# Attention with a relation bias: score matmuls moved from 128-row to 64-row TensorE tiles

## What is computed

```python
attn_scores = jnp.einsum('bihd,bjhd->bhij', q, k) / scale
li = x @ rel_W[:, :d].T
lj = x @ rel_W[:, d:].T
logits = li[:, :, None, :] + lj[:, None, :, :] + rel_b
relation_probs = jax.nn.softmax(logits, axis=-1)
bias = jnp.einsum('bijk,hk->bhij', relation_probs, logical_bias)
attn_scores = attn_scores + gate * bias
attn_weights = jax.nn.softmax(attn_scores, axis=-1)
out = jnp.einsum('bhij,bjhd->bihd', attn_weights, v)
```

## Time and profile before

| | |
|---|---|
| median of three runs | 5008.73 us |
| the profiled execution | 5018.32 us, its span 5016.4 us |
| busy PE, DVE, ACT, POOL | 89%, 76%, 67%, 41% |
| mean DMA rate over the span | 114 GB/s |
| PE instructions (matmul, weight load) | 74128, 74128 |

### The profile page before, as it was taken

One profiled execution on the slowest core, in us unless ns is written; L12 is line 12 of the kernel. 1 busy time (PEld: TensorE's weight loads), 2 busy tenths in 40 slices (PEclk: granted clock), 3 DMA queues, 4 the chain that ended last, 5 costly groups with the idle time before them and its releaser, 6 DMA issues. The chain is left out here.

```text
span 5016.4 us, 183232 instructions
## 1 busy us (share of the span) xinstructions
PE 4458.2 (89%) x74128; PEld 3458.1 (69%) x74128; DVE 3821.7 (76%) x6309; ACT 3380.7 (67%) x4458; POOL 2057.0 (41%) x1809
## 2 busy tenths in 40 slices
PE   6459999999999999999999999999999996289992
PEld 3227777777777777777777777777777785267771
DVE  4388888888888888888888888888888843167773
ACT  2017887888787788877877787888888882044440
POOL 0114444444444444444444444444444442433335
PEclk9659999999999999999999999999999998589996
DMA  7514544544555445554454455454554456244434
GB/s 96 82 33 112 118 113 111 118 112 115 113 112 112 111 114 116 113 118 110 114 114 112 109 113 116 113 119 115 115 114 111 112 114 178 79 146 149 150 137 113
DMA packets 496919, 573.65 MB, mean 114 GB/s; under 512 B 136360, under 2 KB 369704, under 8 KB 492096
## 3 DMA queue, kind: packets, MB, share of 16 engines
q1 hardware_dynamic: 486880, 543.96, 46.5%
q0 software_dynamic: 6144, 16.79, 1.1%
q10 hardware_dynamic: 3040, 0.98, 0.1%
HBM read 305.10 MB, written 46.65 MB: 70 GB/s over the span
## 5 line engine op out<-in xcount | busy, mean ns | idle before, releaser
L734 DVE TENSOR_REDUCE b_mxp<-b_mx 128x1 f32<-128x512 f32 x4096 | 2635.4, 686 | 559.0 <-PE b_mx L835 508.9
L703 ACT ACTIVATE b_pr<-b_sc 128x1024 f32<-128x1024 f32 x2048 | 1986.5, 1021 | 697.0 <-PE b_sc L824 689.2
L814 PE MATMUL b_sc<-b_qm,kst 128*128 128x128 f16 x16384 | 1272.3, 220 | 54.3 <-ACT b_pr L703 42.0
L824 PE MATMUL b_sc<-b_cm,b_rst 112*128 112x128 f16 x16384 | 1264.5, 220 | 42.8 <-DMA b_rst<-b_rhi 35.5
L814 PEld LDWEIGHTS b_sc<-b_qm,kst 128*128 128x128 f16 x16384 | 971.6, 98 | 283.7 <-issue 229.5
L860 PE MATMUL b_acc<-b_pr,vp 128*32 128x128 f32 x32768 | 1124.1, 277 | 27.3 <-issue 26.9
L824 PEld LDWEIGHTS b_sc<-b_cm,b_rst 112*128 112x128 f16 x16384 | 1012.0, 98 | 49.4 <-DMA b_rst<-b_rhi 40.4
L860 PEld LDWEIGHTS b_acc<-b_pr,vp 128*32 128x32 f32 x32768 | 839.2, 110 | 265.2 <-ACT b_pr L703 190.2
L636 POOL TENSOR_TENSOR b_ex<-b_ex 128x512 f32<-128x512 f32 x512 | 654.7, 1279 | 680.8 <-ACT b_ex L682 680.8
L835 PE MATMUL b_mx<-kst,b_qx 64*128 64x512 f16 x4096 | 819.4, 397 | 92.1 <-DVE b_mxp L734 76.9
L642 POOL CAST b_rhi<-b_ex 128x512 f16<-128x512 f32 x512 | 312.8, 611 | 1293.0 <-ACT b_ex L690 1244.5
(11 more groups left out here) (144 smaller groups left out, 1726.0 us busy)
## 6 DMA issues: line engine op xcount, KB each, us to landing
b_dj<-key_logits SPq DMA_DIRECT2D x256, 768.0 KB, 7.9
b_rst<-b_rhi SPq DMA_DIRECT2D x2048, 64.0 KB, 3.2
b_rst<-b_rlo SPq DMA_DIRECT2D x1024, 64.0 KB, 3.1
c_w1r<-in_L_ffn_W_dram SPq DMA_DIRECT2D x23, 1024.0 KB, 4.9
c_w2r<-in_L_ffn_W_dram SPq DMA_DIRECT2D x23, 1024.0 KB, 4.8
expert_tokens<-c_zeros SPq DMA_DIRECT2D x23, 512.0 KB, 6.8
c_xb<-expert_tokens SPq DMA_DIRECT2D x23, 512.0 KB
expert_results<-c_y SPq DMA_DIRECT2D x23, 512.0 KB, 2.9
```

What stands on the lines that cost most here:

```text
L703: nc.scalar.activation(pr[:, jt % 2, half, :], sc[:, half].rearrange("p a b -> p (a b)"), ACT.Exp).then_inc(s["p_ready"], 1)
L734: nc.vector.tensor_reduce(mxp[:, head, part:part + 1], mx[:, (bank + ab) % MX_RING, :], AX.X, ALU.max).then_inc(s["mx_used"], 1)
L814: pe.matmul(sc[:, half, side, p * P:p * P + P], kst[:, pair, jt * P:jt * P + P], qm[:, par, :, pair, side * IS:side * IS + IS], start=(p = ...
L824: ins = pe.matmul(out, rst[:, u % 2, b, j0:j0 + P], cm[:, par, half, b], start=False, stop=(b % (NB // 2) == NB // 2 - 1), skip_group_chec ...
```

## The change

The score part of a step is cut differently. The products use 64-row tiles: head a of a pair on rows 0 to 63, head b on rows 64 to 127, each matmul with 64 moving columns (half of the queries), 32 matmuls a step; q is no longer padded with zeros. The relation part is also on 64 rows: 16 groups of 4 rows (three parts and a row of ones) for 8 queries, again 32 matmuls a step with 64 columns, one 64-row tile for each half of the queries. The halves of ACT's Exp are now even and odd heads. The relation matmuls come first, each half behind `p_ready`, then all products; the second half of the products waits on a new semaphore `relation_done`; `scores_ready` rises twice at the very end. `pe_pv` runs in one go behind both halves.

Around it: the relation logits for both terms come as two rows for each half of the partitions, so `dj` is 512 KB a unit and the two 512-wide Exp become one 1024-wide Exp; `sp_r` has 6 copies of 128 KB a unit, spread over rows at a step of 4 partitions, and issued in three portions that wait for `scores_ready` at steps 0, 1 and 2 of the unit; the coefficient map has 512 columns on 128 partitions instead of 1024 on 112; `pool_sum` runs ahead of `pool_c` and `pool_parts` behind it; the q copies move to units 2 and 3; the constants of a chunk take 11 DMAs instead of 4, and the bound 2 instead of 1. Token order is plain, so loads and stores of 8 DMAs become one each, and the 48 stores of `c_values` become 4.

```diff
-NB, BI = 8, 16
+NB, BI = 8, 8
+PARTS = 4
-C_MAPS = (12, 13)
+C_MAPS = (13, 14)
...
-                for b in range(NB):
-                    sp.dma_start(x[BI * b:BI * b + BI, 8 * q:8 * q + 8, :],
-                                 by_block(hidden)[b // 4, b % 4, :, 8 * q:8 * q + 8, :]).then_inc(x_in[q], 16)
+                sp.dma_start(x[:, 8 * q:8 * q + 8, :],
+                             hidden.rearrange("o (t p) d -> (o p) t d", p=P)[:, 8 * q:8 * q + 8, :]).then_inc(x_in[q], 16)
...
-            for part, t in ((0, chi), (1, chi), (2, clo)):
+            for part, t in enumerate((chi, clo)):
                 for k in range(2):
-                    for b in range(NB):
-                        sp.dma_start(c_dram[:, part, k].rearrange("x (i b) h -> b i x h", b=NB)[b],
-                                     t[BI * b:BI * b + BI, k]).then_inc(stored, 16)
+                    sp.dma_start(c_dram[part].rearrange("a k i x h -> k a i (x h)")[k],
+                                 t[:, k].rearrange("p x h -> p (x h)")).then_inc(stored, 16)
...
-        dj = sb("dj", [P, 2, 3, JU])
-        rst = sb("rst", [ROWS, 2, NB, JU], F16)
-        qm = sb("qm", [P, 2, 2, PAIRS, P], F16)
-        cm = sb("cm", [ROWS, 2, 2, NB, HH, BI], F16)
+        dj = sb("dj", [P, 2, 2, JU])
+        rst = sb("rst", [P, 2, NB, JU], F16)
+        qm = sb("qm", [P, 2, PAIRS, P], F16)
+        cm = sb("cm", [P, 2, 2, NB, PAIRS, BI], F16)
...
-            sp.dma_start(cval[0:M_ROW, par].rearrange("r b h -> r (b h)"),
-                         c_dram[bass.ds(x, 1)].rearrange("o a k (i b) h -> (o a k i) (b h)", b=NB)).then_inc(s[f"cval_in{par}"], 16)
             for side in range(2):
-                sp.dma_start(const[IS * side:IS * side + IS, par, 0:4],
...
+                for part in range(3):
+                    sp.dma_start(cval[IS * side + part:IS * side + IS:PARTS, par],
...
+                for k in range(2):
+                    sp.dma_start(const[IS * k:IS * k + IS, par, side],
...
-        def sp_r(sp, x, u, k):
-
-            sp.wait_ge(s["lo_ready"], 16 * x + 2 * u + k + 1)
-            waited(sp)
-            for side in range(2):
-                for part, t in enumerate((rhi, rlo, rhi)):
-                    row = 32 * part + BI * k
-                    sp.dma_start(rst[row:row + BI, u % 2, NB // 2 * side:NB // 2 * side + NB // 2, :],
-                                 t[IS * side:IS * side + IS, 2 * (u % 2) + k, :]).then_inc(s[f"r_in{u % 2}"], 16)
+        def sp_r(sp, x, u, side, parts):
+
+            if 0 in parts:
+                sp.wait_ge(s["lo_ready"], 16 * x + 2 * u + side + 1)
+                waited(sp)
+            for part in parts:
+                t = rlo if part == 1 else rhi
+                sp.dma_start(rst[IS * side + part:IS * side + IS:PARTS, u % 2],
+                             t[:, 2 * (u % 2) + side, :]).then_inc(s[f"r_in{u % 2}"], 16)
...
-                    sp.wait_ge(s["scores_ready"], STEPS * c + max(SPU * u, 1))
-                    waited(sp)
-                    for k in range(2):
+                    for step, (side, parts) in enumerate(((0, (0, 1)), (0, (2,)), (1, (0,)), (1, (1, 2)))):
+                        if step != 2:
+                            sp.wait_ge(s["scores_ready"], STEPS * c + max(SPU * u + 2 * min(step, 2), 1))
+                            waited(sp)
                         if u + 1 < UNITS:
-                            sp_r(sp, c, u + 1, k)
+                            sp_r(sp, c, u + 1, side, parts)
...
+                    if u == M_UNIT and not last:
+                        sp_m_out(sp, c + 1)
+                        sp_m_in(sp, c + 1, 1 - par)
...
-            for i, sign in enumerate(((1.0, 1.0), (-1.0, 1.0))[k]):
-                nc.scalar.activation(ex[:, k, i], dl[:, k, i], ACT.Exp, scale=sign).then_inc(s["e_ready"], 1)
+            nc.scalar.activation(ex[:, k].rearrange("p n j -> p (n j)"), dl[:, k].rearrange("p n j -> p (n j)"),
+                                 ACT.Exp).then_inc(s["e_ready"], 1)
...
+        def pe_relation(pe, c, par, jt, half):
+
+            u, j0 = jt // 4, jt % 4 * P
+            if jt == 0:
+                pe.wait_ge(s["c_made"], 2 * c + half + 1)
+            if jt % 4 == 0 and half == 0:
+                pe.wait_ge(s[f"r_in{u % 2}"], 96 * (UNITS // 2 * c + u // 2 + 1))
+            if not (isinstance(c, int) and c == 0 and jt == 0):
+                pe.wait_ge(s["p_ready"], STEPS * c + 2 * jt + half - 1)
             for b in range(NB):
+                for side in range(2):
+                    rows = slice(IS * side, IS * side + IS)
+                    out = sc[:, half, side, :].rearrange("p (h i) -> p h i", h=PAIRS)[:, :, b * BI:b * BI + BI]
+                    ins = pe.matmul(out, rst[rows, u % 2, b, j0:j0 + P], cm[rows, par, half, b], start=(b == 0), stop=False,
+                                    skip_group_check=True)
+            return ins
+
+        def pe_products(pe, c, par, jt):
+
+            if jt == 0:
+                pe.wait_ge(s["q_in"], 64 * c + 64)
+            for turn in range(2):
+                if turn:
+                    pe.wait_ge(s["relation_done"], NT * c + jt + 1)
+                for pair in range(PAIRS):
+                    for ab in range(2):
+                        side, rows = (turn + ab) % 2, slice(64 * ab, 64 * ab + 64)
+                        ins = pe.matmul(sc[:, ab, side, pair * IS:pair * IS + IS], kst[rows, pair, jt * P:jt * P + P],
+                                        qm[rows, par, pair, side * IS:side * IS + IS], start=False,
+                                        stop=(pair == PAIRS - 1), skip_group_check=True)
+                        if pair == PAIRS - 1 and turn == 1:
+                            ins.then_inc(s["scores_ready"], 1)
+
+        def pe_scores(pe, c, par, jt):
+
+            pe_relation(pe, c, par, jt, 0)
+            pe_relation(pe, c, par, jt, 1).then_inc(s["relation_done"], 1)
+            pe_products(pe, c, par, jt)
```

More of the change, by code:

```diff
@@ L51 @@
 EXP_MAX = 43.0
-M_ROW = 6 * BI
-ROWS = M_ROW + BI
 MXU = S // 512
@@ L508, in sp_q @@
                     row = 64 * ab + 32 * part
[L509 to L518, removed]
+                    sp.dma_start(t[row:row + 32, par].rearrange("r q t -> r (q t)"),
+                                 parts_twice(x, ab, part)).then_inc(s[arrived], 16)
@@ L578, in _ @@
                 sp_dj(sp, u)
-            for k in range(2):
-                sp_r(sp, 0, 0, k)
+            sp.wait_ge(s["ones_made"], 1)
+            for side in range(2):
+                sp_r(sp, 0, 0, side, range(3))
             sp_m_out(sp, 0)
@@ L606, in chunk @@
                         sp_att(sp, c)
-                        if more:
-                            sp.wait_ge(s["c_made"], 2 * c + 2)
-                            waited(sp)
-                            sp_qx(sp, c + 2, par)
+                    if u == 2 and not last:
+                        sp_q(sp, c + 1, 1 - par, qm, "q_in")
+                    if u == 3 and more:
+                        sp.wait_ge(s["c_made"], 2 * c + 2)
+                        waited(sp)
+                        sp_q(sp, c + 2, par, qx, f"qx_in{par}")
                     if u + 1 == UNITS and more:
@@ L801, in _ @@
             dve_out(dve, NT)
-        def pe_scores(pe, c, par, jt, half):
+        def pe_relation(pe, c, par, jt, half):
             u, j0 = jt // 4, jt % 4 * P
-            if jt == 0 and half == 0:
-                pe.wait_ge(s["q_in"], 64 * c + 64)
-            if not (isinstance(c, int) and c == 0 and jt == 0):
-                pe.wait_ge(s["p_ready"], STEPS * c + 2 * jt + half - 1)
-            for p in range(4):
-                pair = 4 * half + p
-                for side in range(2):
-                    pe.matmul(sc[:, half, side, p * P:p * P + P], kst[:, pair, jt * P:jt * P + P],
-                              qm[:, par, :, pair, side * IS:side * IS + IS], start=(p == 0), stop=False,
-                              skip_group_check=True)
             if jt == 0:
@@ L819, in pe_scores @@
             if jt % 4 == 0 and half == 0:
-                pe.wait_ge(s[f"r_in{u % 2}"], 192 * (UNITS // 2 * c + u // 2 + 1))
+                pe.wait_ge(s[f"r_in{u % 2}"], 96 * (UNITS // 2 * c + u // 2 + 1))
+            if not (isinstance(c, int) and c == 0 and jt == 0):
+                pe.wait_ge(s["p_ready"], STEPS * c + 2 * jt + half - 1)
             for b in range(NB):
-                side, i0 = b // (NB // 2), b % (NB // 2) * BI
-                out = sc[:, half, side, :].rearrange("p (h i) -> p h i", h=HH)[:, :, i0:i0 + BI]
-                ins = pe.matmul(out, rst[:, u % 2, b, j0:j0 + P], cm[:, par, half, b], start=False,
-                                stop=(b % (NB // 2) == NB // 2 - 1), skip_group_check=True)
-            ins.then_inc(s["scores_ready"], 1)
+                for side in range(2):
+                    rows = slice(IS * side, IS * side + IS)
[21 more added lines that the diff above has]
```

(22 more changed lines are left out.)

152 lines of the change are left out of this document (75 added, 77 removed).

## The result

The changed kernel has a median of 5024.8 us over five runs (5015.02 to 5028.63), against 5006.49 us for the kernel before on the same chip. The ratio is 1.0039, with a 95% interval of 1.0022 to 1.0055: 0.4% slower, so in practice no change. The forecast was 4715, 6% faster. The profiled execution has a span of 5013.2 us.

A forecast was written before the change was run, and what follows sets the result against it. PE bounded the kernel at 3.55 us a step; afterwards instruction supply, 3.43 us a step, gives a stage of 3548 us (-267), with -27 outside: 4724 us profiled, 4715 median. Range 4420 to 5150; the forecast's own range 4600 to 4950.

The forecast's parts named there:

- The other stops: Attention stage: POOL-sum wait goes; last relation copies take 4.4 to 7.6 of 6.9 us, taken as met.
- The instruction supply: PE's instruction fetch: 0.816 packets a step, one every 4.2 us, sets the step at 3.43 us.
- The list of signs: What the profile would show if right (PE stops for "issue") or wrong, including PE waiting for b_rst.
- the rivals: Other outcomes: supply keeps up, 4427 us, chance 0.2; row tiles don't overlap, 4918, 0.13; supply worse, 5338, 0.25.
- The array's side: PE's 64 score matmuls: row tiles overlap in pairs, 0.90 us instead of 1.80; PE's step 2.45 us.
- The 25 ns: Skill page's least spacing of matmul starts; taken over both tiles, the loop would be 3.48 us, the time 4765.
- ACT and DVE: Their step limits: ACT about 3.1 us with the 1024-wide Exp at 1.02, DVE 3.15, hiding a 2.95 us loop.
- ACT's wait for POOL's sum: ACT's waits in the attention stage, 82.7 us in 23 chunks, 3.6 us a chunk, would go.
- Outside the stage: Before and after attention: stores save 30.7 us, extra DMAs add 8.8, merged loads and stores save 5; together -27.
- The sum: Stage 3548 us, 267 less, and -27 outside it: 4724 us profiled, 4715 as a median.
- The worse supply: PE's instruction queue: a block every 4.95 us makes the step 4.04 us, +358, 5338 us; chance 0.25.

The follow-up runs named there:

- e1: Changed kernel with the key-logit copy of a unit cut into two DMAs with an outermost dimension of 64: 4695.74 us, ratio 0.9362.
- e5: e1 with 16 relation matmuls of 128 columns a step instead of 32 of 64, part of the relation bias left out: 4493.69 us, ratio 0.8924.
- e4: Kernel before, only its key logits laid out by unit and copied as a broadcast to 128 partitions: 4975.78 us.
- e8: Changed kernel with the key-logit copy in two DMAs, each with an outermost dimension of 2: 5157.16 us, ratio 1.03.
- e9: Changed kernel with the key-logit copy in two DMAs, each with an outermost dimension of 4: 4709.99 us, ratio 0.9406.
- e3: Kernel before, only its key logits laid out by unit and copied with an outermost dimension of 2: 6607.03 us.

## Why the prediction was wrong

**The step that failed** is in "The other stops": two issues at 0.6 us and 3.2 to 6.4 to land, 4.4 to 7.6 us of the 6.9 that the last relation copies of a unit have, "I take that as met". From their release to PE's start it took 13.0 us at key tile 16, on average over all chunks, and 12.1 at 20. Of this 4.6 and 3.6 us passed before SP issued the first of the two (0.13 in e1), 0.9 and 0.8 until it issued the second, and 7.5 and 7.7 until PE went on. The stops cost 12.0 us a chunk, where the upper end was to add 6. The row was the landing time in a kernel whose key logits use all engines and only its q copies two, and I carried it over to one whose key logits use two as well. The same slip is in "The instruction supply": "the key logits a third fewer bytes, so there is a little less in the way". I costed the new copy by its bytes. By its shape it takes some six times as long (10.2 us against 1.7). The working looked at what each copy moves and at when it is issued, and at no place at how many DMA engines it runs on. The list of signs did name the one that came, PE waiting for b_rst, but it had no chance among the rivals.

The forecast of -6% was thus made for e1, and e1 lets its other steps be judged:

- **The array's side** was right. In the changed kernel, in a step without a wait:

```profile
2008.03 0.75 PE L815 MATMUL b_sc<-b_cm,b_rst 64*128 64x64 f16 x32
2008.62 0.64 PE L829 MATMUL b_sc<-b_qm,kst 64*128 64x64 f16 x32
2009.12 0.39 PE L848 MATMUL b_mx<-kst,b_qx 64*128 64x512 f16 x2
```

  The starts are 0.59 and 0.50 apart: 1.09 us for 64 matmuls, 17 ns each, where I said 0.90 and 14, and 1.80 before. In the quickest quarter of the steps the 64 take 0.97 us or less, 15 ns each. There is no 0.10 in front of the maxima pair. The 25 ns that I weighed from the Trainium skill, "TensorE: Matmul & The Clock Gate", section "Wait — 56ns, not 53.3ns?", do not hold over two row tiles: 64 of them would take 1.60.
- **The instruction supply** came out as forecast in e1. 649 packets in 2800 us and 809 steps are 0.802 a step (0.816 forecast) and 4.31 us apart (4.2); 0.802 x 4.31 = 3.46 us a step, against 3.43. The waits for "issue" are 278 us, with 12.8 at L849, or 0.34 us a step: what lies between 3.46 and DVE's 3.15. e5 bears it out by taking instructions out. That the fetch is hidden behind dispatch, as the Trainium skill has it in "Runtime: NRT & Kernel Launch", section "Instruction fetch mechanics", does not fit: PE did wait, and fewer instructions helped. In the changed kernel this limit was covered by a slower one.
- **ACT and DVE**: 3.15 us as DVE's own limit is borne out by e5, 3.264 with the chunk's end (0.03) and the last waits in it. The merged Exp takes 1.06 (1.02 forecast).
- **ACT's wait for POOL's sum** is gone as forecast: 3.9 us in the stretch for the 82.7 of the earlier trace rows.
- **Outside the stage** I said -27. The first scores Exp starts at 336.88 instead of 354.73, -17.8 us, where 30.7 less 8.8 make 22 of the forecast; the matmuls for v did start at 160.77 for 194.99 (about 165 forecast). The part behind the stage is 5013.2 - 4184.0 = 829.2 us for 847.0, another -17.8, which I had put at a few us; what it comes from was not looked into. Together -35.6.
- **The sum.** Stage: 4184.0 - 336.9 = 3847 us, 32 more than before instead of 267 less; with -35.6 that is -3 for the profiled executions, and +0.4% in the medians. For e1 the stage is 3542.5 (forecast 3548). One figure of the working was off by itself: blocks of 3.95 us give 4502 by the same sum, not the 4600 at which the forecast's own range begins.

**The rivals.** The worse supply, the only one of them slower than before (5338 us), had the right sign by luck and the wrong place: PE hardly waited for "issue". What the list lacked was a rival in the DMA engines. I had gone by issue times and the average DMA share, 50% before, and let the falling load stand as evidence against trouble there.

## What to carry to other kernels

Give every DMA whose shape a change touches an outermost dimension that 16 divides, on both sides, as e1 and e4 have it, and cost it by the engines it runs on, not by its bytes: a load that is even on average says nothing about the fullest engine. In a profile, look for a long flat stretch of the DMA row at one or two tenths while an engine waits for data. And when a large gain fails to appear, look for one new wait before doubting the reasons for the gain: here one copy hid all of it.

## What the runs showed of the hardware that was not expected

- A copy with an outermost dimension of 2 ran on two DMA engines, the same two for separate DMAs (e8): 64 x 159 ns for 512 KB. An outermost dimension of 4 was enough here (e9 within 0.3% of e1).
- SP took longer to issue a DMA for the two full engines: 2.04 us on average for a q copy (up to 9.73 us for four), and 0.67 for the same copy in e1. That delayed the relation copies behind them in its queue, which had nothing to do with these copies.
- TensorE paid twice for each stop: after 4.19 us without work the next groups ran at the lower clock level (1.04 for 0.63 us, PV 1.63 for 1.08). The granted clock over the stretch was 0.93, in e1 0.99, and in e3, with the longest stops, 0.86.
